# Local attention over six layers: the feed-forward work of a chunk dealt out differently over the four steps that carry it

## The reference

```python
def attn_layer(x, Wqkv, qs, ksc, Wo):
    q, k, v = heads(x @ Wqkv)
    q, k = l2norm(q) * qs, l2norm(k) * ksc
    q = q * cos * scale + rotate_half(q) * sin * scale
    k = k * cos / scale + rotate_half(k) * sin / scale
    return local_attention(q, k, v) @ Wo

def ffn_layer(x, g, bln, W1, b1, W2, b2):
    mu, var = x.mean(-1), ((x - mu) ** 2).mean(-1)
    xn = (x - mu) / jnp.sqrt(var + 1e-05) * g + bln
    a, gate = jnp.split(xn @ W1 + b1, 2, -1)
    return a * jax.nn.gelu(gate, approximate=False) @ W2 + b2

for i in range(6):
    x = attn_layer(shift_tokens(x), ...) + x
    x = ffn_layer(shift_tokens(x), ...) + x
```

## Time and profile before

| | us |
|---|---|
| three runs | 4048.76, 4052.15, 4038.02 |
| their median | 4048.76 |
| the profiled execution | 4040.43 |
| its span | 4038.7 |
| TensorE matmul busy | 3679.2 (91%) |
| VectorE busy | 3039.7 (75%) |
| ScalarE busy | 2528.0 (63%) |
| GpSimd busy | 1253.9 (31%) |

### The profile page before, as it was taken

One profiled execution on the slowest core, in us unless ns is written; L12 is line 12 of the kernel. 1 busy time (PEld: TensorE's weight loads), 2 busy tenths in 40 slices (PEclk: granted clock), 3 DMA queues, 4 the chain that ended last, 5 costly groups with the idle time before them and its releaser, 6 DMA issues.

```text
span 4038.7 us, 121758 instructions
## 1 busy us (share of the span) xinstructions
PE 3679.2 (91%) x50424; PEld 2018.2 (50%) x50424; DVE 3039.7 (75%) x5112; ACT 2528.0 (63%) x3810; POOL 1253.9 (31%) x1107
## 2 busy tenths in 40 slices
PE   6789999999999989998999999999998899999998
PEld 2355555555555555554644555555554333333333
DVE  7788988888888888885636666666666777777772
ACT  6456766666666666765436565555654576767775
POOL 0465666656556655650100000000000211111121
PEclk8899999999999999997589999999999899999999
DMA  2123222223223222221000000000001311111100
GB/s 74 33 65 82 70 66 78 69 65 81 73 64 82 69 72 75 70 60 31 22 1 3 4 4 5 4 5 2 4 7 39 89 21 21 21 21 21 26 2 11
DMA packets 84943, 162.89 MB, mean 40 GB/s; under 512 B 26874, under 2 KB 36970, under 8 KB 83138
## 3 DMA queue, kind: packets, MB, share of 16 engines
q1 hardware_dynamic: 84146, 154.45, 14.7%
q10 hardware_dynamic: 240, 0.44, 0.1%
HBM read 39.70 MB, written 7.73 MB: 12 GB/s over the span
## 4 chain that ended last, share of the span: by engine, by line
PE 38%; issue 23%; POOL 19%; DVE 11%; ACT 7%; POOLq 0%; ACTq 0%; DVEq 0%; SPq 0%; DMA 0%
POOL arena L1523 9%; POOL arena L1527 7%; PE banks L1863 6%; PE banks L3180 5%; PE banks L1826 3%; ACT arena L3343 2%; DVE arena L2033 2%; PE banks L1844 2%; PE banks L3138 2%; PE banks L3154 2%; PE banks L1882 2%; POOL arena L1507 2%; DVE arena L2052 1%; DVE arena L1381 1%; DVE arena L1372 1%
## 5 line engine op out<-in xcount | busy, mean ns | idle before, releaser
L3429 DVE TENSOR_REDUCE arena<-banks 128x2 f32<-128x1024 f32 x512 | 614.1, 1223 | 189.9 <-PE banks L3145 89.2
L3343 ACT ACTIVATE arena<-banks 128x1024 f32<-128x1024 f32 x512 | 521.3, 1024 | 215.3 <-PE banks L3161 103.9
L1523 POOL TENSOR_TENSOR arena<-arena 128x512 f32<-128x512 f32 x384 | 425.2, 1129 | 634.0 <-DVE arena L1381 626.5
L1527 POOL TENSOR_TENSOR arena<-arena 128x1024 f32<-128x1024 f32 x192 | 533.1, 2776 | 15.1
L2033 DVE CUSTOM_DVE_ANT_0 arena<-arena,banks 128x512 f32<-128x512 f32 (+3 forms) x640 | 361.8, 603 | 143.4 <-issue 138.2
L972 PE MATMUL banks<-arena 128*128 128x512 f32 x768 | 371.2, 628 | 26.5 <-issue 13.9
L1971 ACT ACTIVATE arena<-banks 128x512 f32<-128x512 f32 (+3 forms) x320 | 168.9, 528 | 335.8 <-PE banks L1845 334.7
L3180 PE MATMUL banks<-arena 128*32 128x256 f32 x4096 | 333.8, 392 | 13.5 <-issue 8.1
L1963 ACT ACTIVATE arena<-arena 128x128 f32<-128x128 f32 (+15 forms) x256 | 328.7, 1285 | 14.3 <-DVE arena L2045 9.7
L2115 POOL COPY arena<-arena 128x512 f32<-128x512 f32 x32 | 19.7, 617 | 991.7 <-DVE arena L2059 991.7
L1826 PE MATMUL banks<-arena 64*128 64x512 f32 (+3 forms) x1280 | 318.4, 573 | 6.6 <-issue 4.5
(11 more groups left out here) (456 smaller groups left out, 7547.9 us busy)
## 6 DMA issues: line engine op xcount, KB each, us to landing
arena<-arena SPq DMA_DIRECT2D x774, 64.0 KB, 2.4
arena<-arena SPq DMA_DIRECT2D x96, 384.0 KB, 3.6
arena<-arena SPq DMA_DIRECT2D x104, 128.0 KB, 3.4
arena<-in_lf_wqkv SPq DMA_DIRECT2D x6, 1024.0 KB, 5.6
arena<-arena SPq DMA_DIRECT2D x8, 512.0 KB, 3.1
arena<-features_k SPq DMA_DIRECT2D x28, 128.0 KB
arena<-in_lf_wqkv SPq DMA_DIRECT2D x6, 512.0 KB, 4.2
arena<-in_lf_wo SPq DMA_DIRECT2D x6, 512.0 KB, 4.0
```

The source lines that it names most:

```text
L1523: nc.gpsimd.tensor_tensor(r[:, :, e * H2:(e + 1) * H2], q[:, j, :, (1 - e) * H2:(2 - e) * H2], s[:, j, 1, e * H2:(e + 1) * H2].unsqueeze(1 ...
L1527: nc.gpsimd.tensor_tensor(a, a, lf_rb, ALU.add).then_inc(S("lf_rot" + x), 1)
L3343: nc.scalar.activation(bi_PT[n % 4], PS[:, 2 * bi_slot("S", n):2 * bi_slot("S", n) + 2].rearrange("p a b -> p (a b)"), ACT.Exp).then_inc(S ...
L3429: nc.vector.tensor_reduce(bi_max[j % 2][:, t, :, c], PS[:, 2 * slot:2 * slot + 2], AX.X, ALU.max).then_inc(S("bi_mx"), 1)
```

## The change

A step's feed-forward work is now named by `lf_work`: nothing at j = 0 (where the down product of the chunk before stays, with the second and third of VectorE's products of that chunk), "norm" at j = 1, "first" at j = 2 and "last" at j = 3. Norm is mean, variance, centring and deviation with the shifted copies. First is the gate products 0 and 1 and the other half of 0; last is the gate product 2 and the other halves of 1 and 2. The third product of these two steps stands between the projection and the second half of the values, behind a wait for the copy of k, and uses bank 4, which belongs to the scores; so the scores of the next step wait for the gelu (after first) or for VectorE's product (after last). ScalarE applies two gelus under one table load in first and one in last. The last layer's final two chunks keep their old form.

```diff
--- before.py
+++ after.py
@@ -256,7 +256,7 @@
                 return (2, 3) if m == 1 else (6, 7)
             if end and c == 3:
                 return ((6, 7), (0, 1), (2, 3))[m]
-            return 6, 7
+            return ((6, 7), (4, 7), (6, 4))[m]
 
         def lf_live(n, end):
             return n >= 0 and not (end and n >= NB)
@@ -264,6 +264,15 @@
         def lf_chunk(s, end):
             c, j = divmod(s - 8, 4)
             return c, j, c >= 0 and not (end and c >= NCH)
+
+        def lf_work(s, end):
+
+            c, j, ffn = lf_chunk(s, end)
+            if not ffn:
+                return c, None
+            if end and c == 2:
+                return c, "norm" if j == 0 else None
+            return c, (None, "norm", "first", "last")[j]
 
         def lf_chunk_before(s, end):
             c = (s - 8) // 4 - 1
@@ -975,19 +984,22 @@
 
             def ffn_taken(s, l, end):
 
-                c, j, ffn = lf_chunk(s, end)
+                c, work = lf_work(s, end)
                 b, ending = lf_chunk_before(s, end)
-                if ffn and j:
-                    pe.wait_ge(S("lf_h"), l * 12 + (3 * c + j))
-                elif ffn:
+                if work == "norm":
                     pe.wait_ge(S("lf_xc"), l * NCH + (c + 1))
+                if work == "first":
+                    pe.wait_ge(S("lf_h"), l * 12 + (3 * c + 1))
+                if work == "last":
+                    pe.wait_ge(S("lf_gelu"), l * 12 + (3 * c + 3))
+                    pe.wait_ge(S("lf_h"), l * 12 + (3 * c + 2))
                 if ending:
                     pe.wait_ge(S("lf_y"), l * NCH + (NCH + b + 1))
 
             def turn_q(n, l, end):
 
                 pe.wait_ge(S("lf_rotq"), l * NB + (n + 1))
-                if n >= 1 and not lf_chunk(n, end)[2]:
+                if n >= 1 and not lf_work(n, end)[1]:
                     pe.wait_ge(S("lf_v"), l * NB + n)
                 ffn_taken(n, l, end)
                 for p in range(8):
@@ -1019,9 +1031,13 @@
                     pe.wait_ge(S("lf_kT"), l * NB + (n + 1))
                     if n >= 3:
                         pe.wait_ge(S("lf_y2"), l * NB + (n - 2))
-                    c, j, ffn = lf_chunk(n + 1, end)
-                    if ffn and j == 0:
+                    c, work = lf_work(n + 1, end)
+                    if work == "norm":
                         pe.wait_ge(S("lf_lnv"), l * NCH + (c + 1))
+                    if work == "first":
+                        pe.wait_ge(S("lf_gelu"), l * 12 + (3 * c + 2))
+                    if work == "last":
+                        pe.wait_ge(S("lf_h"), l * 12 + (3 * c + 3))
                     if n == 0:
                         pe.wait_ge(S("lf_zeroed"), 1)
                     pe.sem_inc(S("lf_masking"), 1)
@@ -1125,27 +1141,39 @@
                     vv(s - 1, l)
                     turn_k(s - 1, l)
 
-                    if ffn or ending:
+                    if work or ending:
                         pe.wait_ge(S("lf_v"), l * NB + s)
                 elif s >= 1:
                     ffn_taken(s - 1, l, end)
                 if ending:
                     down(b, l)
-                if ffn and j:
-                    up(c, j - 1, l, 0)
+                if work == "first":
+                    up(c, 0, l, 0)
+                if work == "last":
+                    up(c, 2, l, 0)
 
                 if lf_live(s - 3, end):
                     values_ready(s - 3, l, end)
-                if ffn and j:
-                    up(c, j - 1, l, 1)
-                elif ffn:
+                if work == "first":
+                    up(c, 0, l, 1)
+                if work == "last":
+                    up(c, 1, l, 1)
+                if work == "norm":
                     mean(c, l)
+                if not work and lf_live(s - 3, end):
+                    pe.sem_inc(S("lf_ready"), 1)
                 if lf_live(s - 3, end):
                     values(s - 3, l, 0)
                 if lf_live(s - 4, end):
                     project(s - 4, l, end)
-                if ffn and j == 0:
+                if work == "norm":
                     var(c, l)
+                if work in ("first", "last"):
+                    pe.wait_ge(S("lf_kT"), l * NB + s)
+                if work == "first":
+                    up(c, 1, l, 0)
+                if work == "last":
+                    up(c, 2, l, 1)
                 if lf_live(s - 3, end):
                     values(s - 3, l, 1)
 
@@ -1273,8 +1301,8 @@
                     act.wait_ge(S("lf_w1_in"), (l + c // NCH) * 32 + 32)
                 nc.scalar.activation(lf_xc, lf_xc, ACT.Identity, scale=lf_vec[:, 0:1], bias=lf_vec[:, 1:2]).then_inc(S("lf_xf"), 1)
 
-            def gate(c, m, l, end=False):
-                if not end or m == 0:
+            def gate(c, m, l, loaded=False, end=False):
+                if not loaded:
                     nc.scalar.preload_act_table_set(GELU_SET)
                 if m == 0 and c % NCH == 0:
                     act.wait_ge(S("lf_b1_in"), (l + c // NCH) * 16 + 16)
@@ -1285,14 +1313,14 @@
                 nc.scalar.activation(lf_G[m][0:k], PS[0:k, lf_pair(c, m, end)[0]], ACT.Gelu, bias=lf_vec[0:k, 5 + m:6 + m]).then_inc(S("lf_gelu"), 1)
 
             def step(l, s, end):
-                c, j, ffn = lf_chunk(s, end)
-                if ffn and j == 0:
+                c, work = lf_work(s, end)
+                if work == "norm":
                     shifted(c, l)
                 if lf_live(s, end):
                     squares(s, l)
-                if s > 8 and lf_chunk(s - 1, end)[2] and j != 1:
+                if lf_work(s - 1, end)[1] in ("first", "last"):
                     nc.scalar.preload_act_table_set(LN_EXP_SET)
-                if ffn and j == 1:
+                if work == "first":
                     affine(c, l)
                 if lf_live(s - 1, end):
                     keep_q(s - 1, l)
@@ -1304,11 +1332,14 @@
                     exps(s - 2, l)
                 if lf_live(s - 1, end):
                     keep_k(s - 1, l)
-                if ffn and j == 0:
+                if work == "norm":
                     square(c, l)
                     deviation(c, l)
-                elif ffn:
-                    gate(c, j - 1, l)
+                if work == "first":
+                    gate(c, 0, l)
+                    gate(c, 1, l, True)
+                if work == "last":
+                    gate(c, 2, l)
                 if lf_live(s - 3, end):
                     keep_o(s - 3, l)
                 if lf_live(s + 2, end):
...
@@ -1437,14 +1468,15 @@
                                                op0=ALU.add, op1=ALU.add).then_inc(S("lf_y"), 1)
 
             def step(l, s, end):
-                c, j, ffn = lf_chunk(s, end)
+                c, work = lf_work(s, end)
                 b, ending = lf_chunk_before(s, end)
                 if ending:
+                    product(b, 1, l)
                     product(b, 2, l)
-                if ffn and j == 1:
+                if work == "first":
                     normed(c, l)
-                elif ffn and j >= 2:
-                    product(c, j - 2, l)
+                if work == "last":
+                    product(c, 0, l)
                 if lf_live(s, end):
                     norm(s, l)
                 if lf_live(s - 2, end):
```

More of the change, by code:

```diff
@@ L1323, in tail @@
                 exps(NB - 1, l)
-                gate(2, 0, l, True)
+                gate(2, 0, l, False, True)
                 keep_o(NB - 2, l)
-                gate(2, 1, l, True)
-                gate(2, 2, l, True)
+                gate(2, 1, l, True, True)
+                gate(2, 2, l, True, True)
                 keep_o(NB - 1, l)
@@ L1334, in tail @@
                 for m in range(3):
-                    gate(3, m, l, True)
+                    gate(3, m, l, m > 0, True)
             lf_steps(act, step, tail)
```

## The result

| | before | after |
|---|---|---|
| runs beside each other on one chip | 4048.76, 4052.15, 4038.02, 4039.91 | 4087.37, 4088.66, 4103.06, 4098.91 |
| median | 4044.34 | 4093.78 |
| profiled execution | 4040.43 | 4087.37 |
| its span | 4038.7 | 4085.6 |

The change makes the kernel slower: ratio 1.0123, 95% interval [1.0092, 1.0154]. A later repetition with the same source gave 4093.05 and 1.0133 [1.0118, 1.0148]. The direction was forecast; the amount, +49 by the medians and +46.9 by the two spans, is two and a half times the +19.0 of the sum, and lies outside the range.

The account below looks back on a forecast made before the run. A closed TensorE-VectorE ring from scaling to scaling bounds the local-attention rounds. 22 rounds at +0.82 make 18.0, less 0.4 in the first, plus 1.4 at the end: +19.0 us, 4059.4 profiled, 4067.8 forecast; range 4042 to 4090.

Parts of the forecast that it names:

- the tail: End of the local-attention branch: the last scores wait for two VectorE products, from 1789.76 to about 1791.2, +1.4 us.
- The ring: Gapless TensorE-VectorE chain from scaling (multiplication by inverse norms) to scaling; products before TensorE's wait are free if they fit, behind it cost their length.
- C: Third step (j = 2) of a round, to the next scaling: late third product adds 0.86, 16.45 to 17.31 us.
- D: Fourth step (j = 3): 16.70 without the shifted copies plus 0.86 for a late product, 17.56 us instead of 16.93.
- Step A: First step (j = 0): loses mean and variance, 16.88 plus a 0.35 wait for GpSimd's rotation of q, 17.23 instead of 18.66.
- Step B: Second step (j = 1): gets mean and variance, nothing in the window before the scaling wait; 17.46 us instead of 16.70.
- first step A: Step A of the first round, without down product: 17.43 to 15.65 us, 0.4 further down than the other rounds' 1.43.
- The hidden third product: Rival: the late product only fills TensorE's idle gaps, 0.90 less a round, 4030 us; chance 0.10 together with the table-load variant.
- the table loads on ScalarE's path: Rival variant: ScalarE's loads bound the round, 1.74 less each, 4011 us; chance 0.10 together with the hidden product.
- No change: Rival: rotation in time (A 16.88) and D like C (17.31), +0.22 a round, +5.8 in all, 4054.6 us; chance 0.22.
- GpSimd did not become the ring: Rival: in step A GpSimd's slower work delays the q or k transposes, 1.72 a round, +38.8, 4088 us; chance 0.13.
- The signs named beforehand: Intervals near 17.2, 17.5, 17.3, 17.6; q/k product 4.97 after C's and D's first values; GpSimd releases A's q transposes, about 0.3.

Follow-up runs that it names:

- late_filler: The kernel before the change with one more product per round in step C, behind the projection, into bank 4; 4068.46 us, ratio 1.0059 to before.
- filler_in_b: The changed kernel with the mean product of step B also computed once ahead of the wait for the scaling, its result overwritten; 4081.29 us, ratio 1.0100 to before.
- after_again: The changed kernel itself run once more, same source, on the chip of the experiments; 4093.05 us, ratio 1.0133 to before.
- extra_load: The changed kernel with one more ScalarE table load in step C, between its two gelus; 4082.08 us, ratio 1.0096 to before.

## Why the prediction was right in its direction and wrong in its size

- **What the sum missed, together:** 46.9 - 19.0 = 27.9, of which the falls are 13.6, the steady rounds 6.0 (24.0 for 18.0, mostly step B), the jumps 6.7, the tail 2.3, and the rest, of either sign, -0.7.
- **The ring and the price of places: right.** The late third product, forecast at 0.86, costs 0.91 (late_filler) and puts C at 17.37 (17.31) and D at 17.52 (17.56). Moving products ahead gains what the window holds and no more.
- **Step A: right in its sum, wrong in the wait.** 17.14 against 17.23. GpSimd's result is there at 772.90 and the q transposes start at 773.24 behind the scores; it is in time. Instead the scores start 3.90 behind the q/k product, not 3.63, as VectorE's addition (L1443), for which the program has the scores wait, ends only at 772.14. The row itself names no releaser.
- **Step B: the term was too small.** 2.50 + 0.95 + 4.97 + 6.63 + 2.41 was 2.60 + 1.05 + 4.98 + 6.73 + 2.41 = 17.77. The 0.95 came from a mean that ran close behind the down products; alone behind a wait a product takes 1.05, as the up product of the earlier trace rows had already shown. Over 22 rounds 0.31 is 6.8 us.
- **The step that failed most:** "Step B gets mean and variance and nothing in the window" was priced as the ring without a product, as if an idle window were only free time. It costs the clock: 13.6 us in this trace, and 12.5 by the medians of after and filler_in_b. None of the rivals had this. The trace of before could have shown it. The prediction priced the first step A, which has an empty window, at 17.43; in the trace it took 20.34, with mean, values and projection at a granted clock of 0.50 behind a wait of 1.09. That interval was summed and never compared with its row.
- **The jumps were not in the sum:** +6.7 in this trace. The pauses differ between kernels and between executions of one source, so part of this may be chance.
- **The tail: too small.** +3.7 for +1.4. The last scores waited for the two VectorE products as forecast, but from the last scaling they start 2.03 later, not 1.4, in both traces of the change. The other 1.7 lie behind them, where the granted clock over 10 us is 0.66 and was 0.83; in after_again the whole stretch is 73.27, only 0.9 over before.

TensorE's rows at the branch's end, where that wait stands:

```profile
1827.41 1.14 PE L1074 MATMUL banks<-arena 64*64 64x32 f32 x64
1831.70 0.41 PE L1047 MATMUL banks<-arena 64*32 64x512 bf16 x8 [3.15 <-DVE arena L1459]
```

- **The rivals.** The hidden third product and the table loads on ScalarE's path are both refuted (late_filler, extra_load). "No change" had the rotation in time, which was true, but D carries its surplus. GpSimd did not become the ring. Its time of 4088 is nearest to the measured one, by another cause.
- **The signs named beforehand:** the intervals and the 4.97 came out, GpSimd as releaser in A did not; TensorE does wait for ScalarE in C and D, 0.16 and 0.17 ahead of the v product, but behind the scores, where the maximum no longer needs it.

## What to carry to other kernels

Find the ring that closes without a gap, and price each move by the side of the wait on which the instruction lands; the sum of an engine's work says nothing while its place decides. Check the price of a rare case, such as a first round, against its own row in the trace before. Before you empty the stretch in which TensorE waits, ask what clock it comes back at: keep a useful product there, and if none is at hand a useless one can pay. In a hand-written loop reckon with a pause at each jump, whose length differs between builds and between executions, and compare variants by their steady steps before trusting a few microseconds of the total.

## What was not expected of the hardware

- An idle time of 1.30 us, the same in every round, was followed by 1.2 GHz in some rounds only, 3 to 11 of 22 by kernel, for 3.07 us more each when full; one product of 1.02 us in it ended that in this step.
- The pause at a jump has two lengths, 3.2 to 3.9 and 4.5 to 5.2 us, and one source showed both at the same jump. With 64 increments at the start of the program all four were short, and the steps A had pauses of up to 1.3 us instead.
- A kernel with the same steady steps to 0.01 us as another (extra_load and after) had a median 11.7 us lower, which its trace does not explain. The three blocks with unchanged source took 2186.1 to 2195.4 us in the traces of before, after and after_again.
